# Row maxima gathered in PSUM, and whole blocks of P added on GpSimd instead of summed on TensorE

## What is computed

```python
x = L0_attn_x                      # 4 x 2048 x 512, fp32
x = x + layernorm(attn(layernorm(x), Wq, bq, Wk, bk, Wv, bv, Wp, bp))
x = x + layernorm(layernorm(x) @ W[idx] + b[idx])   # idx: argmax of logits and noise, 8 matrices

# attn: 16 heads of 32, causal, and every fourth key is never seen
att = einsum('bhtd,bhsd->bhts', q, k) / sqrt(32)
att = where(mask == 0, -inf, att)  # mask: s <= t and s % 4 != 3
y = einsum('bhts,bhsd->bhtd', softmax(att), v)
```

## Time and profile before

| | us |
|---|---|
| median of 3 runs | 2431.74 |
| lowest, highest | 2428.77, 2431.99 |
| the profiled execution, its own time | 2432.43 |
| span in its profile | 2430.6 |
| PE busy in the span | 2284.5 |
| ACT, DVE, POOL busy | 1748.0, 1725.1, 1558.4 |
| mean granted TensorE clock | 0.979 of full |

### The profile page before, as it was taken

How to read it: one execution, slowest core, us unless ns; L and a number is a source line. 1 busy time by engine, 2 the same in 40 slices (tenths; PEclk the granted TensorE clock), 3 DMA queues, 4 the chain that set the end, 5 groups by cost and what they waited for, 6 DMA issues and landing times.

```text
span 2430.6 us, 43417 instructions
## 1 busy us (share of the span) xinstructions
PE 2284.5 (94%) x14996; PEld 959.5 (39%) x14996; DVE 1725.1 (71%) x4774; ACT 1748.0 (72%) x3206; POOL 1558.4 (64%) x1440
## 2 busy tenths in 40 slices
PE   4899999999999998998999998999799999999897
PEld 2444433433444443433344443343244444333332
DVE  7777787675568777778267768778827677677774
ACT  7568677678767777677866867767677686776683
POOL 3247567788647567588943758668865565776644
PEclk9899999999999999999999999999999999999998
DMA  7213121121233212112141312102113221301001
GB/s 197 72 42 84 33 60 52 28 69 46 56 83 72 59 48 62 30 43 51 37 100 50 85 43 62 57 23 56 40 35 98 75 60 41 85 23 32 17 14 44
DMA packets 224358, 137.49 MB, mean 57 GB/s; under 512 B 146730, under 2 KB 196618, under 8 KB 224138
## 3 DMA queue, kind: packets, MB, share of 16 engines
q1 hardware_dynamic: 222310, 134.65, 21.8%
q10 hardware_dynamic: 1828, 0.07, 0.0%
HBM read 39.69 MB, written 16.78 MB: 23 GB/s over the span
## 4 chain that ended last, share of the span: by engine, by line
PE 68%; DVE 13%; ACT 8%; issue 6%; POOL 4%; DMA 1%; SPq 0%; POOLq 0%; ACTq 0%; DVEq 0%
PE acc L1310 12%; PE acc L1274 11%; PE acc L1294 10%; PE acc L1245 9%; PE acc L1246 8%; PE acc L1247 8%; PE acc L1325 7%; ACT P L962 5%; DVE MHL L1055 3%; DVE MP L1044 3%; DVE acc L1040 3%; POOL P L824 2%; PE acc L1298 2%; DVE STA L1021 1%; PE acc L1250 1%
## 5 line engine op out<-in xcount | busy, mean ns | idle before, releaser
L962 ACT ACTIVATE P<-acc,EX 128x512 f32<-128x512 f32 (+2 forms) x1920 | 1078.1, 640 | 297.7 <-PE acc L1298 138.4
L824 POOL TENSOR_TENSOR P<-P 128x512 f32<-128x512 f32 x732 | 908.6, 1276 | 102.0 <-PE acc L1310 72.4
L1044 DVE TENSOR_REDUCE MP<-acc 128x1 f32<-128x512 f32 (+1 forms) x1088 | 719.5, 679 | 212.2 <-PE acc L1274 208.8
L1040 DVE CUSTOM_DVE_ANT_0 acc<-acc,CB 128x96 f32<-128x96 f32 (+7 forms) x1024 | 449.9, 456 | 253.0 <-PE acc L1274 249.4
L1274 PE MATMUL acc<-KST,QST 96*128 96x512 f16 (+10 forms) x2112 | 592.7, 336 | 38.8 <-DVE MP L1040 21.5
L1294 PE MATMUL acc<-QST,KST 98*128 98x512 f16 (+2 forms) x1920 | 587.1, 357 | 32.4 <-DVE MP L1040 15.4
L1310 PE MATMUL acc<-P,V 128*32 128x512 f32 (+2 forms) x3840 | 435.5, 548 | 1.3 <-ACT P L962 1.1
L1274 PEld LDWEIGHTS acc<-KST,QST 96*128 96x128 f16 x2112 | 194.7, 98 | 352.1 <-issue 60.3
L1294 PEld LDWEIGHTS acc<-QST,KST 98*128 98x128 f16 x1920 | 183.5, 98 | 292.3 <-ACT P L962 55.8
L815 POOL TENSOR_TENSOR QKL<-SC,QKH 128x384 f16<-128x384 f32 (+1 forms) x128 | 136.3, 1065 | 211.8 <-ACT QKH L937 211.5
L803 POOL TENSOR_TENSOR RR<-RR,NHALF 128x1 f32<-128x1 f32 x256 | 144.0, 566 | 183.7 <-DVE NM L1026 183.3
(11 more groups left out here) (152 smaller groups left out, 3010.2 us busy)
## 6 DMA issues: line engine op xcount, KB each, us to landing
QST<-QKH SPq DMA_DIRECT2D x128, 128.0 KB, 3.2
XR<-in_L_attn_x_dram SPq DMA_DIRECT2D x60, 256.0 KB, 2.8
out_dram<-XR SPq DMA_DIRECT2D x60, 256.0 KB, 2.1
KST<-QKH SPq DMA_DIRECT2D x128, 96.0 KB, 2.6
XB<-in_L_attn_x_dram SPq DMA_DIRECT2D x48, 252.0 KB
QST<-QKL SPq DMA_DIRECT2D x64, 128.0 KB, 3.3
KST<-QKL SPq DMA_DIRECT2D x64, 96.0 KB, 2.7
XB<-in_L_attn_x_dram SPq DMA_DIRECT2D x20, 256.0 KB, 3.4
```

The source lines that it names most:

```text
L824: e.tensor_tensor(P[:, acc, a, :], P[:, acc, a, :], P[:, buf, a, :], ALU.add).then_inc(g_s, 1)
L962: e.activation(P[:, p_buf[u, g, sb_], a, t0:512], bank(*step)[:, t0:512], ACT.Exp, scale=EX[:, 1:2]).then_inc(a_e, 1)
L1040: e.tensor_tensor_reduce(out=ps, in0=ps, in1=MASKM[:, 512 - n:512], scale=1.0, scalar=-3.0e38, op0=ALU.add, op1=ALU.max, accum_out=maxima( ...
L1044: e.tensor_reduce(maxima(u, g)[:, r, a, ci:ci + 1], bank(*s)[:, 0:n], AX.X, ALU.max).then_inc(v_m, 1)
```

## The change

- `peaks` writes its 16 maxima into columns 256 to 271 of a PSUM bank instead of `MX`, and the two instructions behind it read them there. The tile `MX` and its MEMSET are gone, and the counts `READY` and `IDH_AT` fall by one.
- The transposes of `shift` go into the same bank, columns 0 to 255, instead of one of the three banks for peaks. The planner has a kind of bank for it, `psH`, at most two, held from `peaks` to ScalarE's copy.
- `on_pe` now gives TensorE the blocks from 3 j on. At j = 2 GpSimd adds blocks 1 to 5 (1 to 4 before), at j = 3 blocks 1 to 8 (1 to 6 before). TensorE sums the accumulator, one whole block and the two narrow ones. At j = 0 and 1 nothing changes.
- Planner's costs: `norm` on ScalarE 1000 ns (820), `peaks` 720 ns (900), and `invert` is declared to need the `out` of the group before, for which the code waited already.

```diff
 def on_pe(j, sb):
-    return sb >= 3 * j - max(j - 1, 0)
+    return sb >= 3 * j
...
-    MOST = {"psX": 2, "psW": 2, "psM": 3, "psS": 4, "psO": 2, "psU": 2}
+    MOST = {"psX": 2, "psW": 2, "psM": 3, "psS": 4, "psO": 2, "psU": 2, "psH": 2}
...
-            add("dve", s - 0.2, 900, ("peaks", u, g), [("dve", "peak", u, g, r, a, ci) for r, a, ci, _ in jobs],
-                [("MHL", ("pe", "shift", u, g))])
-            add("pe", s - 0.2, 300, ("shift", u, g), [("dve", "peaks", u, g)], [("psM", ("act", "shift", u, g))])
+            add("dve", s - 0.2, 720, ("peaks", u, g), [("dve", "peak", u, g, r, a, ci) for r, a, ci, _ in jobs],
+                [("MHL", ("pe", "shift", u, g)), ("psH", ("act", "shift", u, g))])
+            add("pe", s - 0.2, 300, ("shift", u, g), [("dve", "peaks", u, g)])
...
-                    e.activation(MROW[:, :], bank(*s)[0:8, 0:256].bitcast(F16), ACT.Copy).then_inc(a_m, 1)
+                    e.activation(MROW[:, :], bank("peaks", u, g)[0:8, 0:256].bitcast(F16), ACT.Copy).then_inc(a_m, 1)
...
                     dv.wait_ge(v_m, at)
-                    e.tensor_reduce(MX[:, i, :, :].rearrange("p r a -> p (r a)"),
+                    mx = bank(*s)[:, 256:272].rearrange("p (r a) -> p r a", a=4)
+                    if order.emptier[s]:
+                        dv.wait_ge(*emptied(*order.emptier[s]))
+                    e.tensor_reduce(bank(*s)[:, 256:272],
                                     maxima(u, g).rearrange("p r a c -> p (r a) c"), AX.X, ALU.max).then_inc(v_m, 1)
...
-                    e.tensor_scalar(MHL[:, i, :, 0, :], MX[:, i, :, :], -1.0 / SM, None, ALU.mult, ALU.bypass).then_inc(v_m, 1)
+                    e.tensor_scalar(MHL[:, i, :, 0, :], mx, -1.0 / SM, None, ALU.mult, ALU.bypass).then_inc(v_m, 1)
...
-                    e.scalar_tensor_tensor(out=MHL[:, i, :, 1, :], in0=MX[:, i, :, :], scalar=-1.0 / SM,
+                    e.scalar_tensor_tensor(out=MHL[:, i, :, 1, :], in0=mx, scalar=-1.0 / SM,
...
-                    half = bank(*s)[0:8, 0:256].bitcast(F16)
+                    half = bank("peaks", u, g)[0:8, 0:256].bitcast(F16)
```

More of the change, by code:

```diff
@@ L163, in moments @@
         self.add("gp", rank, 600, ("rstd", k, u, r), [("dve", "stats", k, u, r), ("dve", "consts")])
-        self.add(self.normer(k, u), rank, 750 if self.normer(k, u) == "dve" else 820, ("norm", k, u, r), [("gp", "rstd", k, u, r)])
+        self.add(self.normer(k, u), rank, 750 if self.normer(k, u) == "dve" else 1000, ("norm", k, u, r), [("gp", "rstd", k, u, r)])
     def normer(self, k, u):
@@ L275, in attend @@
                         + ([(who, "add", u, g, added(j)[i - 1], a)] if i else [("pe", "pv", u, g, 0)]))
-            add("dve", s + 0.95, 1600, ("invert", u, g), [("pe", "sum", u, g, last)])
+            add("dve", s + 0.95, 1600, ("invert", u, g), [("pe", "sum", u, g, last)]
+                + [("dve", "out", *divmod(s - 1, 4))] * (s > 0))
             add("dve", s + 0.95, 610, ("out", u, g), [("dve", "invert", u, g), ("pe", "pv", u, g, last)],
@@ L519, in sandwich_block @@
         MP = sb("MP", [128, 2 * 16 * sum(most_chunks(j) for j in range(NJ))], F32)
-        MX = sb("MX", [128, 2, 4, 4], F32)
         MHL = sb("MHL", [128, 2, 4, 2, 4], F16)
@@ L579, in sandwich_block @@
                (slice(7, 8), None, slice(7, 8)))
-        READY, IDH_AT, FOLDED = 8, 9, 19
+        READY, IDH_AT, FOLDED = 7, 8, 19
         BIAS = 9 * 16
@@ L601, in sandwich_block @@
         DV = counted(order.dve, lambda s: {
-            "choose": ("p", 4 if s[-1] else 2), "consts": ("c", 8), "ident": ("c", 1), "wmax": ("p", 1), "bmax": ("p", 3),
+            "choose": ("p", 4 if s[-1] else 2), "consts": ("c", 7), "ident": ("c", 1), "wmax": ("p", 1), "bmax": ("p", 3),
             "allmax": ("p", 2), "scales": ("p", (16, 12, 6)[s[-1]] if s[0] == "scales" else 0), "wlow": ("w", 4 if s[0] == "wlow" and s[1] < 2 else 1),
@@ L987, in _ @@
                     e.memset(R3[:, :, :], 0.0).then_inc(v_c, 1)
-                    e.memset(MX[:, :, :, :], 0.0).then_inc(v_c, 1)
                 elif kind == "ident":
```

## The result

The changed kernel takes **2353.2 us** (median of 4 runs, 2350.2 to 2354.7), against 2431.9 for the kernel before, measured beside it. The ratio is 0.9674, with a 95% interval of 0.9658 to 0.9691. The forecast was 2373 us, range 2348 to 2412.

A forecast was written before the change was run, and what follows sets the result against it. PE time was taken as the bound, with GpSimd setting j = 3 after the change. 2432.4 - 63.5 - 48.8 + 46.7 + 7.2 = 2374.0, less 0.7 for the median: 2373 us, range 2348 to 2412.

The forecast's parts named there:

- The holds (-63.5): VectorE's scaling of maxima waits during GpSimd adds; PSUM maxima remove 46.8 us of standing PE and 16.7 us of half clock.
- the bound: Limit on the gain from ending the waits of VectorE's MHL instructions: at most 63.5 us, unnoticed shorter waits giving nothing.
- eight stretches: Stretches behind long L1055 executions where PE was busy 0.1 of 46.9 us; basis of the 46.8 us standing term.
- What ends a hold: Each long L1055 followed ends within 0.3 us of the end of GpSimd's run of adds, not of one add.
- inner range: Whole kernel's time between 2360 and 2395 us, around the forecast 2373, given 60%.
- rival D: At j = 3, saved PE sums are kept in part, half of 48.8 us comes back: 2349 us; 14%.
- The remark on L1057: The old kernel's second MHL instruction reads two SBUF tiles and stretches to 1.286 us, about one add.
- The moved blocks (+5.1 together): 48 blocks from PE to GpSimd: -48.8 for sums, +46.7 PE idle at j = 3, +7.2 for more matmul changes.
- PE's busy time 40 us less: Sign, over the whole kernel, that the forecast is right: PE's busy time falls by 40 us.
- A: Gaps between GpSimd's runs of adds at j = 3 stay at 13 us, adding 77 us: 2450 us; 8%.
- B: VectorE's MHL instructions wait even with PSUM maxima, up to 39 us beside longer runs of adds: some 2556 us; 3%.
- C: PE's clock falls in the j = 3 stages bound by GpSimd, losing 63 us, half covered by idle time: 2405 us; 13%.

The follow-up runs named there:

- e8_old_sbuf: e2_psum with order, banks and waits kept, but the 16 maxima in an SBUF tile again: 2436.1 us, 1.0009 to the kernel before.
- e2_psum: The kernel after with the old division of blocks between TensorE and GpSimd, planned anew, maxima still in PSUM: 2347.0 us, 0.9637 to the kernel before.
- e1_form: The kernel before, order kept, with only L1055 turned into a SCALAR_TENSOR_TENSOR with two SBUF inputs: 2440.9 us, 1.0016 to the kernel before.
- e9_second: The kernel after, with only the second instruction writing MHL reading its maxima from SBUF, through a reduction of its own: 2544.0 us, 1.0449.
- e3_sbuf: The kernel after, order, banks and waits kept, with the maxima in an SBUF tile again: 2572.3 us, 1.0566 to the kernel before.

## Why the prediction was right, and where it was off

**The holds (-63.5): right mechanism, too small.** Measured 89 us with one order for both (e8_old_sbuf, e2_psum). The step that failed is the bound "-63.5, since shorter holds that PE did not notice give nothing". I had priced eight stretches behind the longest holds and taken the rest for unnoticed. The sums over the whole traces tell otherwise. From before to e2_psum PE stands 58.3 us less, where I had 46.8, and works 43.3 us less at half clock, where I had 33.5; at half that is 21.7 instead of 16.7. The last 7.6 us are busy time that I had no term for. "Elsewhere PE hardly stands after the start" was wrong too: PE stood 99.3 us outside the eight stretches, of which 30.3 lie in five holes at the start and the end. The bound was an end taken from the cases I had looked at, not a limit.

**What ends a hold: read too narrowly.** I had written that each long L1055 ends with its run of adds. The one at 1753.76, which lies over a stretch of the earlier trace rows, outlasted the adds (to 1760.10) by 2.0 us and ended with the L828 behind them. The step from "not one add" to "many instructions" was right; what ends a hold is the 128x1 instruction or the pause.

**The inner range was missed.** The 60% for 2360 to 2395 did not come in. The measured 2353 is inside the stated range because that range reached down for rival D, whose mechanism did not occur. That part is luck.

**The remark on L1057 was a misreading** without effect on the sum. "Stretches to 1.286 us, about one add" is true of its record, but not of its form: e1_form and e9_second show the same form held 9.6 and 16.8 us. What comes second in a pair hides its own exposure. L1087 pointed the right way, with a PSUM operand and no wait, but it was weaker evidence than "in 64 executions, beside the same adds" says: only 16 of the 64 overlap an add of P at all. The kernel after settles it: 31 of the 64 executions of L1057, the TENSOR_SCALAR, begin during an add, and all take 173 to 175 ns.

Two rules can be set beside this. The Trainium skill's page "VectorE: DVE Perf Modes", section "Why PSUM operands drop a tier", rules out the 2-port mode for a PSUM operand; the trace fits, with 0.175 us at most in both lines, though it does not tell the mode. The Trainium skill's page "SBUF — State Buffer", section "Who interferes with whom", says that the one that issues first has the shared ports for its whole instruction and that the other is blocked. By that a wait would be one instruction long; the runs disagree for these two lines, with 9.6, 16.8 and 17.1 us.

**The moved blocks (+5.1 together): right, in total and by place.** From e2_psum to the kernel after the medians rise by 6.2 us and the spans by 9.3; the intervals of the two ratios overlap, so not even the sign is certain. The three windows of e2_psum are:

```profile
446.20:619.00 172.80, 171.34 (x1112) 68.12 (x1110) 106.50 (x283) 143.32 (x255) 153.96 (x137) 1.00 0.19 49
1005.60:1179.60 174.00, 172.50 (x1115) 67.03 (x1113) 103.90 (x276) 141.61 (x254) 154.37 (x137) 1.00 0.20 49
1571.10:1740.40 169.30, 168.76 (x1091) 65.02 (x1083) 99.69 (x253) 138.80 (x249) 151.62 (x134) 1.00 0.17 45
```

I had taken 173 each without the holds and 195.5 after, +67.3 together; measured 516.1 and 584.5, +68.4. Outside the windows I had -48.8 - 20.6 + 7.2 = -62.2; measured 9.3 - 68.4 = -59.1.

**How PE's idle time shows: not as I had said.** PE stands 17 us more than in e2_psum (104.9 against 87.8), not 46.7. And its busy time falls by 7.8 us, though 48 block sums are gone. The groups of scores (L1296) and sums (L1327) over the whole execution tell where it went: count, busy us, mean ns, idle before. First e2_psum:

```profile
L1296 PE MATMUL acc<-QST,KST 98*128 98x512 f16 (+2 forms) x1920 | 581.9, 355 | 16.2 <-DVE MP L1039 7.2 <-ACT P L962 4.3 <-DMA QST<-MROW 2.5
L1327 PE MATMUL acc<-P,ONES 128*32 128x512 f32 (+2 forms) x2304 | 231.8, 501 | 1.7 <-ACT P L962 1.6
```

Then the kernel after:

```profile
L1296 PE MATMUL acc<-QST,KST 98*128 98x512 f16 (+2 forms) x1920 | 595.3, 355 | 28.3 <-ACT P L962 15.1 <-DVE MP L1039 8.1 <-DVE MP L1043 2.1
L1327 PE MATMUL acc<-P,ONES 128*32 128x512 f32 (+2 forms) x1920 | 187.1, 492 | 1.8 <-POOL P L824 1.3 <-ACT P L962 0.2
```

The sums lose 44.7 us as priced. PE's work at half clock, 45.5 us against 28.6, takes back up to 8.5 us. And 1920 scores of the same 355 ns cover 13.4 us more, because they overlap less. A stretch of the kernel after shows it:

```profile
1640.79 0.39 PE L1276 MATMUL acc<-KST,QST 96*128 96x512 f16 x1
1641.02 0.38 PE L1296 MATMUL acc<-QST,KST 98*128 98x512 f16 x1
1641.24 0.52 PE L1276 MATMUL acc<-KST,QST 96*128 96x320 f16 x2
...
1642.41 0.38 PE L1276 MATMUL acc<-KST,QST 96*128 96x512 f16 x1
1642.76 0.39 PE L1296 MATMUL acc<-QST,KST 98*128 98x512 f16 x1
```

Packed, the next matmul starts 0.22 us on (1641.02 to 1641.24). At 1642.41 it starts 0.35 us on, a wait of 0.13 us that counts as busy, since the row's 0.38 covers it. Start-to-start distances of 0.5 us and more add up to 186 us in e2_psum and 241 after: +55, of which 50 lie in the three windows. That is near the 58.8 us above the line; that the two are the same time is argued, not shown. "PE's busy time 40 us less" came out (37.1), but 29.3 of that came with the maxima, 21.7 of it by the clock. It was no test of the moved blocks.

**The rivals.** A (the gap between runs of adds stays, 2450): the gaps are 2.7 to 7.1 us, below its 10.8. B (the PSUM form is held too, some 2556): 0.175 us; its mechanism is real, and e3_sbuf, which gives up the PSUM form, measured 2572. C (the clock falls, 2405): it does fall, but little. The granted clock is at half for 3.4 us at a time five times in or next to the j = 3 stages (at 465.6, 639.7, 1155.1, 1721.7 and 1776.3), and PE works 45.5 us at half clock in all, 28.6 in e2_psum, so at most 8.5 us. PE's waits are many and short there, with no hole above 2.0 us between the start and the last unit. D (the saved sums kept in part, 2349) is near the measured number for another reason: its sign was windows no longer than 193 us, and two of the three are 196. Nor were the sums kept: against e2_psum the moved blocks gained nothing.

## What to carry to other kernels

When a tiny instruction shows a worst case many times its best, price it by an experiment that keeps the order, and not by the few worst cases. Here the operand's move to PSUM was worth 89 us of 2436. When work is moved to a neighbouring engine, add up that engine's work in the stage that has the least room, and stop below full: here seven blocks (96 to 97% busy) gained 36 us over six and four, and the eighth (98 to 100%) lost 42. As long as no second engine is full, rank variants by start-to-start sums of the bounding engine's list, since its busy share hides short waits and half clock. The kernel after, with the lowest sum and not the lowest time, shows where that ends.

## What the runs showed of the hardware

- A 16-element TENSOR_SCALAR or SCALAR_TENSOR_TENSOR on VectorE whose tensor inputs all lie in SBUF can wait over many back-to-back GpSimd instructions: 9.6 us beside runs of up to 24 adds, 17.1 us beside runs of 32. All 69 waits above 1.4 us ended in front of a 128x1 instruction of GpSimd or at a pause of it.
- A 16-element TENSOR_REDUCE in SBUF right ahead of them took 0.204 us at most in 64 executions. A 128x512 add on VectorE waited no more than 1.1 us in 43 executions beside GpSimd. Why some of the small instructions get in at the first boundary and others do not stays open.
- With a PSUM input the same two instructions ran at 0.173 to 0.175 us in all 64 executions each. PSUM added nothing to their time.
- The cost of the holds grows faster than the adds, 732 to 912: 89 us with six blocks, 219 us with eight. Most of it is PE standing, 68.7 and 178.6 us. Its work at 1.2 GHz behind the holds (70.5 and 109.4 us, against 28.6 and 45.5 without them) accounts for 21 and 32 us.
